# Scan setup, its constants, first rows and first state moved into the front of a two-layer kernel

## The reference, cut to what matters

```python
h = silu(x_normed @ down_w + down_b)                  # 256 wide, H = 2 heads of f = 128
XQ, XK, XV = h @ wq, h @ wk, h @ wv                   # cut into 32 mini batches of K = 16 tokens
eta = token_idx * sigmoid(h @ lr_w + lr_b) / f        # token_idx = max(1/(1..16) + tok_idx, 0)
def step((W, b), (xq, xk, xv, et)):                   # 32 steps, in order
    grad = ln_fused_l2_bwd(xk @ W + b, xv - xk, gw, gb)
    attn = tril(xq @ xk.T)
    z = xq @ W - et * attn @ grad + b - tril(et) @ grad
    return (W - (et_last * xk).T @ grad, b - sum(et_last * grad)), xq + ln(z, gw, gb)
out = scan(step, (W1, b1), ...)                       # then ln, @ wo, ln, @ up_w + up_b
```

## Time and profile before

| what | us |
|---|---|
| median of 3 runs | 509.59 (509.56 to 510.45) |
| the profiled execution: its own time | 512.14 |
| the profiled execution: its span | 510.4 |
| PE, PEld, DVE busy | 411.2, 272.3, 308.0 |
| ACT, POOL busy | 294.8, 194.5 |
| mean granted clock of TensorE | 0.903 of full speed |

### The profile page before, as it was taken

How to read it: one execution, slowest core, us unless ns; L and a number is a source line. 1 busy time by engine, 2 the same in 40 slices (tenths; PEclk the granted TensorE clock), 3 DMA queues, 4 the chain that set the end, 5 groups by cost and what they waited for, 6 DMA issues and landing times. The chain is left out here.

```text
span 510.4 us, 10303 instructions
## 1 busy us (share of the span) xinstructions
PE 411.2 (81%) x3168; PEld 272.3 (53%) x3168; DVE 308.0 (60%) x1067; ACT 294.8 (58%) x710; POOL 194.5 (38%) x274
## 2 busy tenths in 40 slices
PE   0799999993689999999996199995499574785991
PEld 0443443431467777777774067774154161665981
DVE  4661623612267777777775236777679997356096
ACT  1256756663257667666674245666369754596544
POOL 0000633701328888888886440000435680000003
PEclk9999999997589999999999558998699967997997
DMA  7110232222212222222213340000000001000002
GB/s 197 42 43 22 64 93 62 85 72 70 65 33 64 65 63 62 62 62 62 62 46 97 86 110 5 2 0 1 0 1 0 1 1 22 2 0 1 0 1 82
DMA packets 35163, 23.05 MB, mean 45 GB/s; under 512 B 10286, under 2 KB 34876, under 8 KB 35132
## 3 DMA queue, kind: packets, MB, share of 16 engines
q1 hardware_dynamic: 34716, 22.55, 16.2%
q10 hardware_dynamic: 416, 0.13, 0.1%
HBM read 13.20 MB, written 9.47 MB: 44 GB/s over the span
## 5 line engine op out<-in xcount | busy, mean ns | idle before, releaser
L344 PE MATMUL bank<-w,hT 128*128 128x385 f32 x128 | 48.5, 505 | 0.0
L872 ACT ACTIVATE w_sb<-bank 128x256 f32<-128x256 f32 (+1 forms) x128 | 44.6, 401 | 0.0
L806 PE MATMUL bank<-w_sb,kqt 128*32 128x128 f32 x1024 | 43.0, 283 | 0.0
L578 DVE TENSOR_TENSOR move<-tw,coup 128x512 f32<-128x512 f32 x12 | 14.2, 1181 | 41.3 <-ACT coup L483 41.3
L344 PEld LDWEIGHTS bank<-w,hT 128*128 128x128 f32 x128 | 22.4, 189 | 30.2 <-issue 20.9
L1135 ACT ACTIVATE std_<-mv_,cst 128x2 f32<-128x2 f32 (+1 forms) x46 | 13.5, 296 | 36.7 <-DVE mv_ L1115 20.2
L1348 POOL TENSOR_TENSOR win<-win,lng 128x512 f32<-128x512 f32 x2 | 2.5, 1264 | 78.6 <-ACT win L1629 78.6
L806 PEld LDWEIGHTS bank<-w_sb,kqt 128*32 128x32 f32 x1024 | 25.4, 110 | 7.9 <-issue 0.4
L604 POOL TENSOR_TENSOR turn<-xnT,coup 128x512 f32<-128x512 f32 x4 | 7.0, 1750 | 54.6 <-ACT coup L483 54.6
L1364 PE MATMUL bank<-xn1T,w1e 128*128 128x512 f32 x32 | 17.7, 676 | 11.1 <-ACT he L1525 10.9
L941 POOL TENSOR_SCALAR xh<-raw,bmv,brs 128x128 f32<-128x128 f32 x32 | 25.4, 793 | 3.0 <-DVE brs L993 2.9
(11 more groups left out here) (294 smaller groups left out, 1222.2 us busy)
## 6 DMA issues: line engine op xcount, KB each, us to landing
rows_scratch<-stage SPq DMA_DIRECT2D x32, 192.5 KB
rows<-rows_scratch SPq DMA_DIRECT2D x32, 192.5 KB, 2.4
attn_scratch<-ob SPq DMA_DIRECT2D x32, 64.0 KB, 1.6
att<-attn_scratch SPq DMA_DIRECT2D x32, 64.0 KB
xt<-in_L_attn_x SPq DMA_DIRECT2D x4, 256.0 KB, 6.1
out<-win SPq DMA_DIRECT2D x4, 256.0 KB, 2.4
cst<-in_constants SPq DMA_DIRECT2D x1, 535.5 KB, 4.2
w<-in_L_attn_wk SPq DMA_DIRECT2D x2, 128.0 KB, 4.8
```

The lines of the kernel that those rows point to most:

```text
L344: mm = nc.tensor.matmul(rows_bank(i, h)[:, 0:RC], hT[:, k, i * P:(i + 1) * P], w4[:, k, h, :], start=(k == 0), stop=(k == 1))
L578: nc.vector.tensor_tensor(move[:, b % 2, :], tws[cyc][:, cols(b)], coup[:, b, :], ALU.mult).then_inc(moved, 1)
L806: mm = nc.tensor.matmul(dst[32 * b:32 * b + 32, 0:F], v[:, at:at + 2 * K], w_sb[:, state, first_slot(b) + h, :], start=False, stop=(h == 1 ...
L872: nc.scalar.activation(w_sb[:, state, at:at + n, :], bank[b][:, 0:n * F].rearrange("f (h g) -> f h g", h=n), ACT.Copy).then_inc(w_done, 1)
```

## The change

The front becomes one block. The setup block of the scan is gone; its parts are in the front. In words, for each engine:

- SP: the late loads follow the projection weights at once, then the five loads of the scan's setup. After the stores of tile 14 it waits for seven stores of the even tiles and loads the rows of steps 0 to 3, then it stores tile 15. The wait for all stores is now ahead of the load for step 4, in the scan.
- PE: transposes go to banks 4 to 7, so the down projection can start without a meeting of the engines. The product that spreads the head rows (`head_constants`) stands between the bias products and the twisted input, in bank 5. `second` for batches 2 and 3 waits until bank 5 is read.
- DVE: each copy of a transposed batch comes after the normalisation of the next batch. The constants (`scan_constants`, 18 instructions) are computed between the folding of `wo` and `up` and the wait for `gf`.
- POOL: clears `kqt` at the very start; after the constants it copies the first state from `w0c` and `bias0` to `w_sb`. ACT does not copy the first state any more.
- In the scan, PE writes state banks 0 and 1 between the transposes of steps 0 and 1, and banks 2 and 3 between the two grams. ACT starts with a square root of a constant, whose result nobody reads. `w_done` counts four less.
- Buffers: the scan's rows, transposed rows, state copies and constants lie in `win` and `wst`; `x1` lies over `xn`, `tw1` in `d0`.

```diff
@@ build
+        m1 = Layer1(nc, sb, sem, ffnT, region1)
+        m0 = ScanSetup(m1, sem)          # lends pieces of win and wst
         layer0_in(nc, a, const, out, locals())
@@ front, DVE
+                    def scan_constants(ch, dve):
+                        dve.wait_ge(bias_mm, 3)
+                        ch.mark(nc.vector.tensor_copy(m0.gr[:], bank[5][:, 0:F]))
+                        ch.mark(nc.vector.tensor_copy(m0.gbr[:], bank[5][:, F:2 * F]))
+                        nc.vector.tensor_copy(m0.b1r[:], bank[5][:, 2 * F:3 * F]).then_inc(biases_read, 1)
...
+                        dve.sem_inc(biases_read, 1)
@@ front, DVE, in the loop over batches of the normalisation
+                        if b:
+                            turned_copy(b - 1)
+                    turned_copy(B - 1)
@@ front, SP
+                    for n, name in enumerate(("ttt_ln_w", "ttt_ln_b")):
+                        sp.dma_start(m0.head_rows[:, n * F:(n + 1) * F], a["L0_attn_" + name]).then_inc(m0.ld, 16)
+                    sp.dma_start(m0.head_rows[:, 2 * F:3 * F], ...b1...).then_inc(m0.ld, 16)
+                    sp.dma_start(m0.tok[:], ...tok_idx...).then_inc(m0.ld, 16)
+                    sp.dma_start(m0.w0[:], ...W1...).then_inc(m0.ld, 16)
                     for i in range(NT):
...
-                    for p in range(2):
-                        sp.wait_ge(stored[p], 32 * (NT // 2))
+                        if i == NT - 2:
+                            sp.wait_ge(stored[0], 32 * 7)
+                            for t in range(RING):
+                                sp.dma_start(m0.rows[:, t, :], ...rows_d[t]...).then_inc(m0.rows_in[t], 16)
@@ front, PE
+                    def head_constants():
+                        pe.wait_ge(m0.ld, 80)
+                        pe.wait_ge(stage_done[0], 2)
+                        pe.wait_ge(lr_done, 3)
+                        nc.tensor.matmul(bank[5][:, 0:3 * F], con("headT", H), m0.head_rows[:], start=True,
+                                         stop=True).then_inc(bias_mm, 1)
...
+                    head_constants()
                     for b in range(B):           # the twisted input
...
+                    pe.wait_ge(biases_read, 5)
                     for b in range(2, B):
                         second(0, b)
@@ front, POOL
+                    nc.gpsimd.memset(m0.kqt[:], 0.0)
+                    pool.wait_ge(biases_read, 6)
+                    nc.gpsimd.tensor_copy(m0.w_sb[:, 0, 0:H, :], m0.w0c[:])
+                    nc.gpsimd.tensor_copy(m0.w_sb[:, 0, H, :], m0.bias0[:])
+                    for b in range(1, B):
+                        nc.gpsimd.tensor_copy(m0.w_sb[:, 0, b * H + 1:b * H + 1 + H, :], m0.w0c[:])
@@ scan: the setup block (L689 to L732) is removed
@@ scan, SP, load(s, p)
+                    if isinstance(s, int) and s == RING:
+                        for parity in range(2):
+                            sp.wait_ge(m0.stored[parity], 32 * (NT // 2))
@@ scan, PE
                 transposes(0, 0)
+                state_bank(0)
+                state_bank(1)
                 transposes(1, 1)
-                base(zbanks[0], keys(0), 0, 0).then_inc(z_mm, 1)
+                base(zbanks[0], keys(0), 0, None).then_inc(z_mm, 1)
                 pe.wait_ge(kt_done, 2)
                 grams(0, 0, pairs=False)
+                state_bank(2)
+                state_bank(3)
                 grams(1, 1)
@@ scan, ACT
-                act.wait_ge(zeroed, 1)
+                nc.scalar.activation(std[:], con("eps6"), ACT.Sqrt)
                 prep(0, 0)
-                for b in range(B):
-                    copy_state(-1, b, 0)
                 prep(1, 1)
```

More of the change, by code:

```diff
@@ L3 @@
+import math
 from contextlib import ExitStack
@@ L273, in layer0_in @@
             stage_done = [sem(f"stage_done{h}", c1) for h in range(H)]
-            stored = [sem(f"rows_stored{p}", c1) for p in range(2)]
+            stored = m0.stored
             N = 512
@@ L484, in couple @@
                                        scale=beta[:, 0:1]).then_inc(coupled, 1)
+                    load(act, down_in, down[:], a["L0_attn_down_w"])
+                    load(act, down_in, down_b[:], col(a["L0_attn_down_b"], 2))
+                    act.wait_ge(cst_in, 16)
+                    for b in range(B):
+                        act.wait_ge(stats_done, b + 1)
+                        s = slice(b * TPB, (b + 1) * TPB)
+                        act.activation(std[:, s], mv[:, s, 1], ACT.Sqrt, bias=con("eps5")).then_inc(std_done, 1)
                     act.wait_ge(down_in, loads[down_in])
@@ L649, in ttt @@
     with ExitStack() as c:
-        rows = sb("rows", [P, RING, RC], c=c)
-        kqt = sb("kqt", [P, RING, 2, B * BW], c=c)
+        m0 = g["m0"]
+        rows, kqt, w_sb, w0c = m0.rows, m0.kqt, m0.w_sb, m0.w0c
+        gr, grf, gbr, g2, ggb, bias0 = m0.gr, m0.grf, m0.gbr, m0.g2, m0.ggb, m0.bias0
+        tim, blkt, headt = m0.tim, m0.blkt, m0.headt
         kd = sb("kd", [P, 2, P], c=c)
@@ L671, in ttt @@
         grad, raw = sb("grad", [P, 2, F], c=c), sb("raw", [P, 2, F], c=c)
-        ld, setup = sem("ttt_loads", c), sem("ttt_setup", c)
-        head_mm, zeroed = sem("head_mm", c), sem("zeroed", c)
-        rows_in = [sem(f"rows_in{p}", c) for p in range(RING)]
+        rows_in = m0.rows_in
         ob_out = [sem(f"ob_out{p}", c) for p in range(2)]
@@ L697, in _ @@
-                for t in range(RING):
-                    sp.dma_start(rows[:, t, :], rows_d[t].rearrange("b h j c -> (b h j) c")[:, 0:RC]).then_inc(rows_in[t], 16)
-            @block.tensor
-            def _(pe):
-                pe.wait_ge(ld, 80)
-                nc.tensor.matmul(prep_bank[:, 0:3 * F], con("headT", H), head_rows[:], start=True, stop=True).then_inc(head_mm, 1)
-            @block.gpsimd
-            def _(pool):
-                nc.gpsimd.memset(kqt[:], 0.0).then_inc(zeroed, 1)
@@ L798, in base @@
                     for half in range(2):
-                        pe.wait_ge(w_done, copied + 2 * half + 2)
+                        if copied is not None:
+                            wait(pe, w_done, copied + 2 * half + 2)
                         if half == 0:
@@ L829, in step @@
                     wait(pe, raw_done, t)
-                    base(zbar_bank, queries(p), p % 2, 4 * t)
+                    base(zbar_bank, queries(p), p % 2, None if isinstance(t, int) and t == 0 else 4 * (t - 1))
                     pe.wait_ge(mask_done, t + 1)
@@ L836, in step, with state_bank @@
                     if left >= 2:
-                        base(zbanks[p % 2], keys((p + 2) % RING), (p + 1) % 2, 4 * (t + 1))
-                for b in range(B):
+                        base(zbanks[p % 2], keys((p + 2) % RING), (p + 1) % 2, 4 * t)
+                def state_bank(b):
                     for h in range(H):
```

265 lines of the change are left out of this document (160 added, 105 removed).

## The result

The changed kernel takes **495.25 us** (median of 4 runs, 494.50 to 497.22) against 510.02 (509.56 to 510.56, 4 runs) for the kernel before in the same session: a ratio of 0.9716, interval 0.9685 to 0.9747. The forecast was 494.0, range 491.2 to 497.2. Six more runs of the same kernel in a later session gave 494.46 (492.57 to 495.32), ratio 0.968 [0.9648, 0.9712].

A forecast was written before the change was run, and what follows sets the result against it. The stretch before the scan was taken as bound by waits, not an engine. Boundary -11.85, prologue -3.5 and front -0.2 sum to -15.55; 509.59 - 15.55 = 494.0 us, range 491.2 to 497.2.

The forecast's parts named there:

- The boundary: Between front and scan: no wait for tile 15's stores and no setup block, scan starts at 121.15; minus 11.85 us.
- the rival of late rows: Scan start: step 0's rows land after 121.2, replacing the removed wait, at most 3.2 us; 497.2 us, chance 0.02.
- The front: Stage before the scan: three terms, the second and third cancelling; minus 0.2 us.
- the down projection: Front, first term: its start moves with the last transposes, minus 0.7 to plus 0.5, taken as minus 0.2 us.
- the late load's wait: Front, second term: first network product no longer waits for the last small load, issued ten microseconds earlier; minus 0.85 us.
- the head product: Front, third term: two PE instructions ahead of the twisted input; plus 0.8 us (0.4 to 1.6).
- The prologue: Scan's start to first product with a gradient: 13.2 to 9.7, minus 3.5 us, bounds minus 1.8 and minus 5.0.
- the likeliest case: Prologue's clock: starts at half, full after some 4.5 us, in `base`; prologue 9.7 us.
- A prologue at half clock throughout: Rival: clock falls and stays low through the prologue, about 11.4 us; 495.7 us in all, chance 0.15.
- the rival of the dearer switch: ScalarE at the scan's start: table switch costs about 1.3 us beyond its row; 495.0 us, chance 0.03.
- The slower steps: Rival: scan tiles in other memory lengthen each step; at 0.6 us a step 512.6 us; slower than before, chance 0.02.
- the bound of 0.79 us for 128 columns: Front, POOL's state copies: dearest step's price for 9 x 128 columns, at most 7.1 us, to 53.8.

The follow-up runs named there:

- the repeated kernel: The changed kernel run again unaltered in the second session, to see what differs between profiles; 494.46 us, ratio 0.968 to the kernel before.
- the loads held back: Changed kernel, but SP holds the late loads until the last transposes are through, still in the single block; 498.07 us, ratio 0.9755 to the kernel before.
- the added wait: Changed kernel with SP's wait for all stores put back at the end of the front; 498.98 us, ratio 0.9771 to the kernel before.
- the constants' block: Changed kernel with head product, constants and POOL's state copies in their own block between front and scan, loads still early; 501.46 us, ratio 0.9831.
- the one with the banks first: Changed kernel with all four state banks written before the first transposes, state copies kept on POOL; 494.30 us, ratio 0.9689 to the kernel before.
- the split front: Changed kernel with the front cut into two blocks before the down projection, late and setup loads in the first; 500.90 us, ratio 0.9812.

## Why the prediction was right

**The boundary** was right in size: from SP's last issue to the scan's first product -11.51, where the working has 120.73 to 121.15, or -11.88. The 0.37 is the meeting, which took 0.75 (to ScalarE's first instruction) to 0.79 (to PE's) instead of 0.3 to 0.5. The stores' wait went nowhere else: the wait ahead of the load for step 4 is not among SP's DMA waits in the scan. The rows were in time, the rival of late rows fell.

**The front** was right in sign, and too small: -1.38 for -0.2. Term by term: the down projection -0.62 (19.82 to 19.20) for -0.2, as it waits for one copy and not for four; the late load's wait -0.85 as predicted, since nothing is waited for at 33.70; the head product +0.91, and +0.83 in the whole stage, for +0.8. A further -0.6 lies in the down projection, 9.33 us to the first row unit instead of 9.92 (9.03 in the repeated kernel), and its cause stays open; so does that of the last -0.15, in the first row units. The mis-sized term is the first. It says that the last batch's normalisation "moves the last transposes by about as much as the wait was long", and takes the last copy for what PE waits for. By the kernel that waits for all four copies that would have been +0.3, inside the term's bounds; the changed kernel waits only for the copy that it reads first. And the terms aren't independent: with the loads held back, the first term and the shorter down projection are lost in the wait for them, so the early loads are worth 2.0 us here (35.71 to 33.70), not 0.85.

**The prologue** took 8.67 for a forecast of 9.7, inside the bounds of 8.2 and 11.4. The clock did what the likeliest case said: down at 119.55 (2.2 us after PE's last product ended at 117.32), back at 123.0. It came back 2.9 us into the block, sooner than the 4.5 I took. The other profiles price the sum's steps: 8.00 us with the clock up throughout (8.2 forecast), 9.18 with the first 4.1 us of the block at half clock (the added wait) and 9.82 with the first 5.5 (the constants' block), and 0.7 for the table load at the full clock (0.8 forecast). Between 9.18 and 9.82 lie about 9.4 for 4.5 us, an estimate, so most of the missing 1.0 is the clock's earlier return. A prologue at half clock throughout, 11.4, was never seen. How the -4.50 divides between the earlier clock, the banks' place and the four state copies that ACT no longer makes is not shown: the copies were not put back in any run. ScalarE's table load stood beside the banks; its root began at 121.40, at once behind the load, so the rival of the dearer switch fell. The Trainium skill, ScalarE: Activation LUTs, section What ACT_TABLE_LOAD costs, counts a drain of about 1380 ns into a switch; neither row here shows one, and neither does a load behind a busy ScalarE (in the kernel before, an activation ends at 403.22, the load takes 403.24 to 404.52, and the next activation starts at 404.54). The clock fell behind 2.82 us of idle PE in the changed kernel and stayed up behind 2.84 in the one with the banks first. The Trainium skill's advice on the clock (TensorE: Matmul & The Clock Gate, section Why this matters for your kernels) warns of longer idle gaps than this one: in the nine profiles here with 2.82 to 2.84 us of idle PE that held in three, and in six the clock was at half in the prologue.

**Missed** was step 0. The working ended at the first product with a gradient and took all that follows as before. But PE waits 1.80 us for the first gradient, and with the clock now high there is something to lose: it fell at 129.8 and step 0 took 1.50 us more. Before, PE idled there 0.92 us, at a clock that had come back at 145.3, 0.9 us before the product. Against the forecast the prologue gives -1.0, this fall +1.5, the front -1.2 and the meeting +0.4: together -0.3. So the number was good to 1.25 us partly because errors of both signs met. In the account, front, boundary, prologue and step 0 sum to -15.89, for a forecast of -15.55.

**The slower steps** didn't come: 4.20 us each behind step 0, and POOL's busy time in the scan is the same (104.41 of 127.5: 103.59 of 126.8). The memory that the tiles lie in made no difference that these profiles show. The range rested on the clock, and rightly: the repeated kernel's six runs alone span 2.75 us.

## What to carry to other kernels

Between two blocks, look for the engine that is last (here SP, with its stores and its loads), and move the serial work of the next block's setup under a stage where the engines wait anyway: 6.75 us of constants and copies cost 0.9 there. In these kernels a block's end makes everyone wait for SP's last DMA issue, so a long list of early loads and a block that ends soon don't go together: the split front lost 6 us by it.

After a part gets shorter, walk the clock to the end of the next stage and not only to the end of the part: behind a wait of PE of 1.80 us at the full clock, five of ten profiles here had a fall, worth 1.5 us. With a few products that nobody reads in the wait, none of three had one; that is a hint and no proof.

## What was not expected of the hardware

The granted clock fell once 2.2 us after PE's last product and again after an idle time of 1.80 us with 1.0 us of products behind it, while the profiled execution of the kernel with the banks first, with the same idle times (2.84 and 1.81 us), kept 1.00 throughout. The same kernel gave a step 0 of 5.70 and of 4.20 us. Whether step 0 had a fall changed between two executions of one kernel, so for stages of this size one profile isn't enough.

POOL's copies were cheaper than the bound of 0.79 us for 128 columns: 0.40 for 256 columns and 0.30 for 128, 1.66 us for all five.
